# An attention kernel with an LSTM-like recurrence: the key projection issued ahead of the query projection, and the wait for the first exponential placed at the queries

## The reference

```python
xn = _layernorm(x, axis=-1)
qkv = xn @ W_qkv + b_qkv                        # 128 -> 3 x 1024
scores = jnp.einsum('nqhd,nkhd->nhqk', q, k)    # 16 heads of 64
attention = softmax(scores / sqrt(64), axis=3)
attn = einsum('nhql,nlhd->nqhd', attention, v).reshape(n, l, 1024) @ W_out + b_out
# recurrence over the 8 sequences: c = f * c + i * g, gates from x_t and c
h = tanh(x @ wo.T + c_final @ uo.T + bo)
x = x + attn + h
```

## Time and profile before

| | |
|---|---|
| three runs, us | 967.5 (median), 966.79, 972.53 |
| profiled execution, us | 967.92 |
| its span, us | 966.1 |
| granted TensorE clock, mean share | 0.986 |
| busy: PE, PEld, DVE, ACT, POOL | 94%, 52%, 60%, 47%, 56% |
| DMA over the span | 13.74 MB, mean 14 GB/s |

### The profile page before, as it was taken

The page is one execution under the profiler, slowest core; times in us unless marked ns, Lnnn a source line. Parts: engine busy times, 40 slices in busy tenths (PEclk is TensorE's granted clock), DMA queues, the critical chain, the costliest instruction groups (busy, mean ns, idle before and its releaser), DMA issues.

```text
span 966.1 us, 14368 instructions
## 1 busy us (share of the span) xinstructions
PE 908.7 (94%) x4901; PEld 499.4 (52%) x4901; DVE 575.1 (60%) x801; ACT 454.3 (47%) x580; POOL 537.0 (56%) x267
## 2 busy tenths in 40 slices
PE   5689999999999999999999999999999999999997
PEld 3465555555555555555555555555555555555442
DVE  6765566546666466646666466646666466646631
ACT  4355455434554445534554445534554455544431
POOL 3023463456665566646665566646665466636661
PEclk9589999999999999999999999999999999999999
DMA  7000000000000000000000000000000000000000
GB/s 218 0 1 1 2 22 1 12 1 12 23 1 11 0 11 22 11 0 11 22 0 11 0 11 22 11 0 11 22 0 11 0 11 22 12 0 13 1 12 11
DMA packets 18635, 13.74 MB, mean 14 GB/s; under 512 B 1298, under 2 KB 16176, under 8 KB 18608
## 3 DMA queue, kind: packets, MB, share of 16 engines
q1 hardware_dynamic: 18608, 13.39, 4.5%
HBM read 6.83 MB, written 2.10 MB: 9 GB/s over the span
## 4 chain that ended last, share of the span: by engine, by line
PE 81%; DVE 9%; ACT 6%; issue 2%; DMA 1%; SPq 1%; ACTq 0%; POOLq 0%; DVEq 0%
PE pv L696 23%; PE st L679 13%; PE st L610 8%; PE mx L661 8%; PE misc L705 6%; PE mx L711 6%; DVE NM L488 5%; PE misc L610 5%; ACT probs L357 5%; PE pv L610 4%; PE st L684 4%; PE mx L610 2%; DMA probs<-in_L_attn_data_dram 1%; PE mx L668 1%; DVE misc L463 1%
## 5 line engine op out<-in xcount | busy, mean ns | idle before, releaser
L488 DVE TENSOR_REDUCE NM<-mx 128x2 f32<-128x1024 f32 x256 | 313.6, 1225 | 215.9 <-PE mx L661 214.1
L254 POOL TENSOR_TENSOR PSUMK<-probs 128x1024 f32<-128x1024 f32 x63 | 149.2, 2368 | 383.5 <-PE misc L705 345.1
L357 ACT ACTIVATE probs<-st 128x1024 f32<-128x1024 f32 x256 | 251.8, 1024 | 186.6 <-PE st L684 184.6
L696 PE MATMUL pv<-probs,VALL 128*64 128x512 f32 x1024 | 231.5, 593 | 0.0
L260 POOL TENSOR_TENSOR PSUMK<-PSUMK,probs 128x1024 f32<-128x1024 f32 x63 | 150.1, 2382 | 10.8 <-ACT probs L357 5.0
L266 POOL TENSOR_TENSOR PSUMK<-PSUMK,probs 128x1024 f32<-128x1024 f32 x63 | 151.1, 2398 | 0.1
L347 ACT COPY AT<-pv 128x512 f32<-128x512 f32 x64 | 37.6, 587 | 240.8 <-PE pv L696 240.8
L696 PEld LDWEIGHTS pv<-probs,VALL 128*64 128x64 f32 x1024 | 72.8, 137 | 144.1 <-issue 138.1
L661 PE MATMUL mx<-KH,QH 64*128 64x512 f32 x512 | 119.3, 461 | 26.7 <-DVE NM L488 20.5
L661 PEld LDWEIGHTS mx<-KH,QH 64*128 64x128 f32 x512 | 49.1, 187 | 117.0 <-issue 75.5
L679 PE MATMUL st<-QH,KH 64*128 64x512 f32 x512 | 108.4, 419 | 0.0
(11 more groups left out here) (170 smaller groups left out, 977.4 us busy)
## 6 DMA issues: line engine op xcount, KB each, us to landing
probs<-in_L_attn_data_dram SPq DMA_DIRECT2D x4, 512.0 KB, 7.4
XSH<-XH SPq DMA_DIRECT2D x8, 256.0 KB, 2.4
XSL<-XL SPq DMA_DIRECT2D x8, 256.0 KB, 2.4
MROW<-TM SPq DMA_DIRECT2D x128, 2.0 KB
RES<-in_L_attn_data_dram SPq DMA_DIRECT2D x8, 256.0 KB, 2.8
out_dram<-RES SPq DMA_DIRECT2D x8, 256.0 KB, 2.3
probs<-in_L_attn_W_qkv_dram SPq DMA_DIRECT2D x3, 512.0 KB, 4.5
WO<-in_L_attn_W_out_dram SPq DMA_DIRECT2D x1, 512.0 KB, 4.8
```

Source lines behind the costliest of these rows:

```text
L254: nc.gpsimd.tensor_tensor(PSUMK[:, :, :], e[:, :, 0, :], e[:, :, 1, :], ALU.add).then_inc(sum_part, 1)
L357: nc.scalar.activation(probs[:, s % 2, :, u, :], st[:, u % 2, :, :], ACT.Exp, scale=SCALE).then_inc(exp_done, 1)
L488: nc.vector.tensor_reduce(NM[:, :].rearrange("p (h b) -> p h b", h=2)[:, :, j], mx[:, :, :], AX.X, ALU.max, negate=True).then_inc(red_done, 1)
L696: last = nc.tensor.matmul(pv[OWN[h], :], VALL[:, kb, s * P + h * HD:s * P + (h + 1) * HD], probs[:, s % 2, h, kb, :], start=(kb == 0), sto ...
```

## The change

Inside TensorE's step, the call of `project` for the keys with its wait for `pv_evac` is moved ahead of the wait for the first exponential of the pair and of the call of `project` for the queries. Nothing else in the program is touched.

```diff
@@ -785,11 +785,12 @@
                     if coming:
                         score_maxima(t + 1, s + 1, 3)
 
+                    if ahead:
+                        wait(pe, pv_evac, t - 1)
+                        project(n, s + 3, DIM, k_done, k_bank)
                     pe.wait_ge(exp_done, 4 * t + 1)
                     if ahead:
                         project(n, s + 3, 0, q_done, q_bank)
-                        wait(pe, pv_evac, t - 1)
-                        project(n, s + 3, DIM, k_done, k_bank)
                     if coming:
                         turn_max(t + 1)
                     if not first:
```

## The result

The changed kernel took 979.86 us in the median of 7 runs (976.77 to 983.08), the kernel before 967.78 in the median of its 7 (966.79 to 972.53). The ratio is 1.0115, 95% interval 1.0088 to 1.0142: about 12 us slower, where +2 had been forecast and at most 975. The profiled execution has a span of 978.1 against 966.1.

What follows compares the result with a forecast made beforehand. TensorE, 81% of the chain, was taken as the bound, already waiting for QL at `scores(2)`. Loop batches +1.7 and last batch +0.5 gave +2.2 us, so a median of 969.7, range 966 to 975.

Steps and rivals of the forecast that it cites:

- the first term: TensorE at the exponential: keys start at M + 0.23 and cover the queries' stall, gaining 0.33 us ahead of the turn.
- M: In each TensorE step, the start of the last maxima matmuls ahead of the projections; the forecast's times count from it.
- the stall of 0.33: TensorE's wait at the queries' second matmul for the first exponential, sized at 0.33 us and expected to go.
- +2.2: Forecast sum in us: +1.7 for six loop batches and +0.5 for the last batch.
- `scores(2)` behind QL decides, not the stall: Third scores block, overwriting the queries' bank, waits for QL; later queries make it 0.16 later in s = 3 and 7.
- the turn's wait for the reduction: The maxima's turn on TensorE must wait for VectorE's reduction, so it gains 0.12 in place of 0.33.
- the 0.1 between s = 3 and s = 4: TM starts 0.1 later after the turn in s = 2, 4, 5, 6, so these lose +0.07 each, not +0.16.
- ScalarE not taking the keys first: ScalarE still takes QH before KH, so keys that are ready sooner have no taker.
- batch 0 unchanged: First batch: no gain at the turn; QH 0.70 later is hidden before the first tanh with 0.18 to spare.
- The rival on the slow side: Queries' chain grows by more than its matmuls: each QL 0.25 later, 39 x 0.25 = 9.8, 975.5 to 979; 8 in 100.
- the unknown costs: Unseen hand-over from QH's end to QL's start and stalled turn: upper ends +3.9 and +1.9, lower end -1.9.
- the figure of the Trainium skill that was weighed ahead: About 131 ns per load and matmul; queries only 0.06 later, sum about -2; set aside for the trace's 0.23.

Runs made afterwards that it cites:

- the run with s = 2 to 7 alone: Against the kernel before, keys ahead of the queries only in s = 2 to 7 of batches 1 to 7: 981.66 us, ratio 1.0145.
- batch 0 alone: Against the kernel before, keys ahead of the queries only in batch 0: 968.18 us, ratio 0.9992.
- the best order tried: Against the kernel before, only the first of three key matmuls ahead of the exponential's wait in batches 1 to 7: 961.14 us, ratio 0.9927.

## Why the prediction was wrong

**The step that failed** is the first term: "the keys' wait is ... over by then, and the keys start at M + 0.23". They start as if at M + 0.42 to 0.43: the second stands at M + 0.65. I took the pace inside a run of like matmuls, 0.23, for the step from 64-row maxima to 128-row keys. The rows to see it by were in the trace before: ahead of the maxima behind the value projection (0.36 to 0.39), of `sums` behind the maxima (0.24 to 0.36) and of the scores behind the gates (0.36), the weight load idles "<- issue" each time, and the prediction has no term for it. One of them, in the step of the earlier trace rows:

```profile
568.17 0.19 PEld L661 LDWEIGHTS mx<-KH,QH 64*128 64x128 f32 x2 [0.36 <-issue]
```

So the stall of 0.33 was mis-sized as a saving: 0.2 of it stays under any order, 0.13 was the exponential's.

**What it does to the sum.** The gap moves QH and QL by 0.2 in each step. In s = 0 and 1 it is absorbed, because the turn waits for the reduction anyway (0.20 and 0.12 forecast, 0.21 and 0.12 measured). That these two came out is in part luck: the six matmuls end at M + 1.81 and not at M + 1.61, just where the reduction lets the turn start. In 39 steps it goes onto `scores(2)` in full: 39 x 0.2 = 7.8, less about 0.16 in each s = 2 of the loop, given back behind `scores(2)`: there the maxima of the kernel before stand behind VectorE's sum of the output (it ends 4.31 after M, they start at M + 4.44), so that start moves by 0.23 only, and the scores behind it by 0.12. +2.2 and 7.8 less 1.0 make +9.0; the traces give 8.4 to s = 4 of batch 7, 0.35 in that step and 0.3 behind it.

**What held.** That `scores(2)` behind QL decides, not the stall; the turn's wait for the reduction (load 0.05 after it, matmul 0.10 more); the 0.1 between s = 3 and s = 4 (0.37 and 0.28 at the load); ScalarE not taking the keys first; batch 0 unchanged but for the clock. QL's start 0.03 to 0.04 after QH's end was sized at 0.05, and QL takes 0.75 in place of 0.73 in these rows.

**The rival on the slow side** had the size (39 x 0.25) and the wrong cause: hand-overs repeat to 0.01. It got 8 in 100. The range left it out; with the gap's 39 x 0.2 = 7.8 among the unknown costs its upper end of 975 would have been near 983.

**The rest.** 12.1 in the medians is 3 more than 9. The fastest runs differ by 10.0 (976.77 and 966.79), and the changed kernel's seven lie in three groups, near 976.8, 979.8 and 982.8, with a granted clock of 0.986 to 0.988, 0.980 and 0.977. The kernel before has such executions too, at 970 and 972. Why the changed one had more of them in its seven, and four of four above 980 in the run with s = 2 to 7 alone, stays open: batch 0 alone doesn't do it.

**Against the figure of the Trainium skill that was weighed ahead** (131 ns between 512-column matmuls): the pace of 0.23 held in every run, and choosing the row was right. The term that was missing is the one that the Trainium skill's rule on tiling modes points at.

## What to carry to other kernels

Moving work into a stall saves only the part of it that the other engine causes; part of this one was a gap of TensorE's own, which any first instruction with another number of weight rows would have met. Size a filler to what is left (here one matmul of three), and ask which later wait hangs on the work that it pushes back. If that work occupies a buffer that is needed next, change the buffer and not the order: that was worth 13 us, where the best order tried gave 7.

## What the runs showed of the hardware

Going from 64-row to 128-row weights or back costs about 0.2 us at the full clock, with or without a wait: the keys' second matmul stands at M + 0.65 in place of M + 0.46, with 0.35 of idle time ahead of the first load. Inside one shape, a satisfied wait costs nothing that the trace shows: in the kernel before the keys, with their wait, start 0.23 after the last query matmul (566.58 behind the 566.35 of the earlier trace rows). And the granted clock fell to 1.2 GHz for a few microseconds in some executions, after TensorE had idled 1.4 to 2.0 us at a time; the fall in s = 5 of batch 7 cost 1.6 us, the one at 66 us cost 3. In other executions the same idle times left it at 2.4 GHz, so they are not enough to bring the fall on.
